# The recovery sums of a FitzHugh-Nagumo step: from GpSimd to ScalarE and VectorE

## The reference

```python
def cell(h, x):                       # layer 0, a GRU over time
    r, z = sigmoid(i_r + h_r), sigmoid(i_z + h_z)
    n = tanh(i_n + r * h_n)
    return (1 - z) * n + z * h
def _derivative(q, p, drive):         # layer 1, FitzHugh-Nagumo, DT = 0.01
    dq = q - q**3 / 3 - p + drive + tanh(q) @ coupling.T + bias
    dp = EPSILON * (q + ALPHA - BETA * p)
# one step: classical RK4 with four derivatives, then q and p are clipped to +-20; q is the output
x = x + gru(cond, x); x = x + fhn(cond, cond, x)
x = x + attention_over_blocks_and_layernorm(x)   # layer 2
x = x + grid_sample_1d(x, cond)                  # layer 3
```

## Time and profile before

| | |
|---|---|
| median of 3 runs | 3843.66 us (3839.34 to 3843.87) |
| the profiled execution | 3839.92 us, its span 3837.5 us |
| TensorE busy (matmul) | 3432.1 us, 89% |
| VectorE busy | 2881.2 us, 75% |
| ScalarE busy | 1870.0 us, 49% |
| GpSimd busy | 2035.7 us, 53% |
| mean granted TensorE clock | 0.845 |

### The profile page before, as it was taken

The page is one execution under the profiler, slowest core; times in us unless marked ns, Lnnn a source line. Parts: engine busy times, 40 slices in busy tenths (PEclk is TensorE's granted clock), DMA queues, the critical chain, the costliest instruction groups (busy, mean ns, idle before and its releaser), DMA issues.

```text
span 3837.5 us, 283786 instructions
## 1 busy us (share of the span) xinstructions
PE 3432.1 (89%) x115469; PEld 3184.2 (83%) x115469; DVE 2881.2 (75%) x17626; ACT 1870.0 (49%) x14495; POOL 2035.7 (53%) x7721
## 2 busy tenths in 40 slices
PE   8988998999999989999999998998999998999977
PEld 4478888888888888888888888888888888888853
DVE  2077777777777777777777777777777777777766
ACT  3245555555555555555555555555555555555543
POOL 0045555555555555555555555555555555555532
PEclk9998888888888888888888888888888888888778
DMA  3000000000000000000000000000000000000001
GB/s 121 22 24 1 1 1 1 1 1 1 1 1 1 1 1 1 1 1 1 1 1 1 1 1 1 1 1 1 1 1 1 1 1 1 1 1 1 1 1 44
DMA packets 9333, 23.44 MB, mean 6 GB/s; under 512 B 556, under 2 KB 600, under 8 KB 8792
## 3 DMA queue, kind: packets, MB, share of 16 engines
q1 hardware_dynamic: 8832, 19.92, 1.4%
q10 hardware_dynamic: 88, 0.02, 0.0%
HBM read 15.75 MB, written 4.19 MB: 5 GB/s over the span
## 4 chain that ended last, share of the span: by engine, by line
PE 80%; DVE 14%; issue 4%; ACT 1%; DVEq 0%; DMA 0%; ACTq 0%; POOL 0%
PE psum L1065 43%; PE psum L1045 31%; PE psum L1017 4%; DVE qnext L811 4%; DVE tpart L771 3%; DVE zdiff L739 2%; PE psum L1165 1%; DVE h L747 1%; DVE psum L811 0%; DVE sq L781 0%; DVE wih L884 0%; DVE q L820 0%; ACT tpart L517 0%; DVE wih L938 0%; DVEq L810 0%
## 5 line engine op out<-in xcount | busy, mean ns | idle before, releaser
L1065 PE MATMUL psum<-tpart,cpl 128*128 128x32 f16 x65536 | 2046.6, 180 | 346.6 <-DVE tpart L771 342.9
L1065 PEld LDWEIGHTS psum<-tpart,cpl 128*128 128x128 f16 x65536 | 1853.8, 98 | 450.4 <-DVE tpart L771 402.0
L1045 PE MATMUL psum<-hpart,whh 128*128 128x32 f16 x49152 | 1507.1, 181 | 7.6 <-DVE hpart L702 7.6
L1045 PEld LDWEIGHTS psum<-hpart,whh 128*128 128x128 f16 x49152 | 1381.2, 99 | 8.5 <-issue 6.2
L517 ACT ACTIVATE tpart<-psum 128x8 f16<-128x8 f32 x3072 | 525.0, 179 | 1127.0 <-DVE psum L811 1045.4
L771 DVE SCALAR_TENSOR_TENSOR tpart<-tfull,tpart 128x8 f16<-128x8 f32 x4096 | 735.1, 183 | 192.9 <-ACT tfull L519 162.6
L811 DVE TENSOR_REDUCE psum<-psum 128x8 f32<-128x24 f32 x3072 | 535.3, 189 | 401.2 <-PE psum L1065 241.3
L389 POOL TENSOR_TENSOR term<-coef,qhat 128x48 f32<-128x48 f32 (+1 forms) x1024 | 276.4, 270 | 511.1 <-ACT qhat L524 510.0
L519 ACT ACTIVATE tfull<-psum 128x8 f32<-128x8 f32 x3072 | 510.0, 175 | 0.0
L401 POOL TENSOR_TENSOR pn<-sums,qhat 128x16 f32<-128x16 f32 x511 | 113.4, 222 | 558.2 <-ACT qhat L524 558.2
L524 ACT ACTIVATE qhat<-psum 128x16 f32<-128x16 f32 x1536 | 324.3, 211 | 0.0
(11 more groups left out here) (148 smaller groups left out, 3602.4 us busy)
## 6 DMA issues: line engine op xcount, KB each, us to landing
xrow<-in_x_dram SPq DMA_DIRECT2D x4, 1024.0 KB, 11.3
out_dram<-space SPq DMA_DIRECT2D x16, 256.0 KB, 2.0
wih<-in_L_cond_W_ih_dram SPq DMA_DIRECT2D x3, 1024.0 KB, 9.6
space<-in_L_cond_W_hh_dram SPq DMA_DIRECT2D x1, 3072.0 KB, 18.7
space<-in_L_cond_coupling_dram SPq DMA_DIRECT2D x1, 1024.0 KB, 19.2
xrow<-in_cond_dram SPq DMA_DIRECT2D x1, 1024.0 KB, 4.8
wih<-in_L_cond_Wk_dram SPq DMA_DIRECT2D x1, 1024.0 KB, 5.4
wih<-in_L_cond_Wo_dram SPq DMA_DIRECT2D x1, 1024.0 KB, 7.7
```

Source lines behind the costliest of these rows:

```text
L1045: mm = pe.matmul(gate_out[part][:, :, :, col:col + B], whh[:, w, k, n * P:(n + 1) * P], copies_in(hpart[:, k, :, :]), start=(col == 0 and ...
L1065: mm = pe.matmul(stage_out[a][:, :, :, col:col + B], cpl[:, w, k, n * P:(n + 1) * P], copies_in(tpart[:, s % 2, k, :, :]), start=(col == 0 ...
```

## The change

GpSimd's work in the loop is given to the two other engines. ScalarE makes each product of the sums by one `Copy` with a constant scale (16 elements each): 4 from `phat`, 4 from `q1`, 3, 2 and 1 from the state in PSUM of stages 0, 1 and 2 (the one `Copy` `qhat` of each stage goes), and the scaled drive. VectorE does all additions, the clip of p, the drive and the output. `coef` and its memsets go. The clip of q becomes two instructions, of another form, one into PSUM and one into SBUF; `cub` and the square of stage 0 lie in PSUM. In stage 3, `base` and `sum_z` change places.

```diff
 # ScalarE
+            def stage_terms(s):
+                for r in range(s + 1, 4):
+                    ins = act.activation(in_halves(qterm[:, s + 1, r, :]), qt, ACT.Copy, scale=STEP[s] * sums_of[r][s + 2])
+                ins.then_inc(qterm_ready[s + 1], 1)
+            def first_terms(v):
+                act.wait_ge(phat_ready, v)
+                for r in range(4):
+                    ins = act.activation(pterm[:, r, :], phat[:, :], ACT.Copy, scale=sums_of[r][0])
+                ins.then_inc(pterm_ready, 1)
+                act.wait_ge(q1_ready, v)
+                for r in range(4):
+                    ins = act.activation(qterm[:, 0, r, :], q1[:, :], ACT.Copy, scale=STEP[3] * sums_of[r][1])
+                ins.then_inc(qterm_ready[0], 1)
+            def scaled_drive(v):
+                act.wait_ge(x1_ready, v)
+                act.activation(uscaled[:, :], x1[:, (v - 1) % 2, :], ACT.Copy, scale=k_c).then_inc(uscaled_ready, 1)
...
+                        if tail <= T:
+                            first_terms(tail)
                         act.wait_ge(q1_ready, tail)
...
                     if s == 1 and gru <= T:
                         gate_input(gru, tail)
                         sigmoid_r(gru)
+                    if s == 1 and tail <= T:
+                        scaled_drive(tail)
 # VectorE
             def clip(v):
+                dve.wait_ge(stage_sum[3][1], v)
+                if v < T:
+                    dve.scalar_tensor_tensor(clipped, qnext[:, :], clampq[:, 0:1], lowest,
+                                             ALU.min, ALU.max).then_inc(clipped_ready, 1)
...
-                dve.tensor_scalar(q1[:, :], qnext[:, :], clampq[:, 0:1], clampq[:, 1:2],
-                                  ALU.min, ALU.max).then_inc(q1_ready, 1)
+                dve.wait_ge(qterm_ready[0], v)
+                dve.scalar_tensor_tensor(q1[:, :], qnext[:, :], clampq[:, 0:1], lowest,
+                                         ALU.min, ALU.max).then_inc(q1_ready, 1)
...
+            def add_terms(s, v):
+                dve.wait_ge(qterm_ready[s], v)
+                if s == 0:
+                    dve.wait_ge(sums0_ready, v)
+                    dve.tensor_tensor(sums[:, :, :], pterm[:, :, :], qterm[:, 0, :, :], ALU.add).then_inc(sums_ready[0], 1)
+                else:
+                    dve.wait_ge(sums_ready[s - 1], v)
+                    dve.tensor_tensor(sums[:, s:4, :], sums[:, s:4, :], qterm[:, s, s:4, :],
+                                      ALU.add).then_inc(sums_ready[s], 1)
...
                 cubic(1, now)
+                first_sums(now)
+                if t >= 1:
+                    new_x(t - 1)
+                add_terms(0, now)
                 base(1, now)
+                if tail <= T:
+                    drive_sum(tail)
...
                 cubic(2, now)
+                add_terms(1, now)
                 base(2, now)
                 if gated_step:
                     sum_nr(gru)
+                if tail <= T:
+                    drive_scaled(tail)
                 sum_stage(2, 0, now)
...
                 cubic(3, now)
+                add_terms(2, now)
                 if gated_step:
                     difference(gru)
+                base(3, now)
+                if gated_step:
                     sum_z(gru)
-                base(3, now)
+                if tail <= T:
+                    add_last(now)
                 sum_stage(3, 0, now)
                 if gated_step:
                     weigh(gru)
+                if tail <= T:
+                    clip_p(tail)
                 sum_stage(3, 1, now)
...
                 clip(now)
                 if tail <= T:
+                    first_drive(tail)
                     split_tanh(0, 1, tail, tanh_ready[3][0], now)
```

More of the change, by code:

```diff
@@ L167, in build @@
         stage_base = psum[:, bank:2 * bank].rearrange("p (a c) -> p a c", a=HALVES)[:, :, 0:HC]
+        scratch_at = bank + 2 * HC
+        cub, square0, clipped, lowest = [psum[:, scratch_at + i * KB:scratch_at + (i + 1) * KB] for i in range(4)]
         stage3 = [triple(0, half), triple(bank + half, half)]
@@ L261, in build @@
         sq_ready = [sem(f"sq_ready{s}") for s in range(4)]
-        qhat_ready = [sem(f"qhat_ready{s}") for s in range(4)]
+        qterm_ready = [sem(f"qterm_ready{s}") for s in range(4)]
+        pterm_ready, clipped_ready = sem("pterm_ready"), sem("clipped_ready")
         cub_ready = [sem(f"cub_ready{s}") for s in range(4)]
         base_ready = [sem(f"base_ready{s}") for s in range(4)]
-        term_ready = [sem(f"term_ready{s}") for s in range(4)]
         sums_ready = [sem(f"sums_ready{s}") for s in range(4)]
@@ L326, in _ @@
                                pattern=[[-1, P]], channel_multiplier=1).then_inc(ident_ready, 1)
-            sums_of = recovery_sums()
-            for src in range(4):
-                for r in range(4):
-                    pool.memset(coef[:, src, r, :], sums_of[r][src] * (STEP[3] if src == 1 else 1.0))
             pool.iota(feature[:, :], pattern=[[-P, K]], base=0, channel_multiplier=-1,
@@ L407, in _ @@
-            for t in range(T):
-                step(t)
-            new_x(T - 1)
             pool.wait_ge(gi_mm, GROUPS)
@@ L753, in _, with drive_sum @@
                 link(ins)
+            def drive_sum(v):
+                dve.wait_ge(h_ready, v)
+                if v >= 3:
+                    dve.wait_ge(x2_ready, v - 2)
+                dve.tensor_tensor(x1[:, (v - 1) % 2, :], xT[:, v - 1, :, :].rearrange("p k b -> p (k b)"), h[:, :],
+                                  ALU.add).then_inc(x1_ready, 1)
             for v in (1, 2):
@@ L764, in _ @@
                 dve.wait_ge(h_ready, v)
+                if v == 1:
+                    drive_sum(1)
             h_high(3)
@@ new lines, in clip, with drive_scaled @@
+                dve.scalar_tensor_tensor(q1[:, :], qnext[:, :], clampq[:, 0:1], lowest,
+                                         ALU.min, ALU.max).then_inc(q1_ready, 1)
+            link(dve.memset(lowest, 1.0))
+            link(dve.tensor_scalar(lowest, lowest, clampq[:, 1:2], None, ALU.mult))
+            dve.tensor_copy(clipped, q1[:, :]).then_inc(clipped_ready, 1)
+            def drive_scaled(v):
+                dve.wait_ge(uscaled_ready, v)
+                dve.tensor_tensor(uhat[:, :], uscaled[:, :], bhat[:, :], ALU.add).then_inc(uhat_ready, 1)
@@ new lines, in first_drive, with new_x, first_sums @@
+            def first_drive(v):
+                dve.wait_ge(uhat_ready, v)
+                dve.wait_ge(phat_ready, v)
+                dve.tensor_tensor(drive0[:, :], uhat[:, :], phat[:, :], ALU.subtract).then_inc(drive0_ready, 1)
+            def new_x(t):
+                dve.wait_ge(q1plain_ready, t + 1)
+                dve.tensor_tensor(xT[:, t, :, :].rearrange("p k b -> p (k b)"), x1[:, t % 2, :], q1plain[:, :],
+                                  ALU.add).then_inc(x2_ready, 1)
+            def first_sums(v):
+                dve.wait_ge(pterm_ready, v)
+                dve.tensor_tensor(pterm[:, 0:3, :], pterm[:, 0:3, :],
+                                  uhat[:, :].unsqueeze(1).broadcast_to([P, 3, KB]), ALU.add).then_inc(sums0_ready, 1)
@@ new lines, in add_last, with clip_p @@
+            def add_last(v):
+                dve.wait_ge(qterm_ready[3], v)
+                dve.wait_ge(sums_ready[2], v)
+                dve.tensor_tensor(pn[:, :], sums[:, 3, :], qterm[:, 3, 3, :], ALU.add).then_inc(pn_ready, 1)
+            def clip_p(v):
+                dve.wait_ge(pn_ready, v - 1)
+                dve.tensor_scalar(phat[:, :], pn[:, :], clampc[:, 0:1], clampc[:, 1:2],
+                                  ALU.min, ALU.max).then_inc(phat_ready, 1)
+            drive_scaled(1)
@@ L823, in _ @@
+            first_drive(1)
             square(1)
@@ L880, in _ @@
                 step(t)
+            new_x(T - 1)
             dve.wait_ge(x2_ready, T)
```

100 lines of the change are left out of this document (24 added, 76 removed).

## The result

The changed kernel takes **4378.16 us** (4 runs, 4376.91 to 4379.42) against 3843.76 us before (4 runs, 3839.34 to 3844.16). The ratio is 1.1393, with a 95% interval of 1.1374 to 1.1413: slower by 534 us, where 4370 was forecast. The whole difference is in the loop. Between two first half-sums of stage 0 there are on average 7.86 us after and 6.82 before, and 511 times 1.04 is 531 us.

The account below looks back on a forecast made before the run. TensorE bound the kernel before, 86% of a step's chain; afterwards mostly VectorE and ScalarE. Six legs sum to 7.69 us, taken as 7.85, 1.03 above 6.82; 511 steps give 526 us more: 4370 us, range 4150 to 4550.

Parts of the forecast that it names:

- A: From stage 0's second half-sum to stage 1's first, through ScalarE's products and VectorE's cubic and additions: 1.74 us, before 1.40.
- B: From stage 1's first half-sum to stage 2's, which is queued behind an addition waiting for ScalarE: 2.10 us, before 1.61.
- D: From stage 3's first half-sum to its second, through sum_z, the sigmoid, weigh and clip_p: 0.71 us, before 0.30.
- the allowance for small waits: Over the whole step, the walk gives some 2% too little, so 7.69 us was taken as 7.80.
- The stall at L799: Between stages 1 and 2, VectorE stands still about 0.5 us ahead of drive_scaled, with stage 2's half-sum queued behind.
- The queue waits at 0.10 instead of 0.03: On VectorE, a late semaphore waited for in the queue costs 0.10 us, not 0.03; five waits, bound -0.35 a step.
- The wide additions at 0.20 and 0.22: VectorE's additions of 48 and 64 elements take 0.20 and 0.22 us; bounds -0.08 to +0.11 a step.
- `clip_p` and the hold: Ahead of stage 3's second half-sum, clip_p holds its follower 0.28 us; bound -0.08 if only 0.20 counts.
- Relief: Rival: GpSimd no longer slows VectorE and the additions fit its free time; 102 us faster, 3740 us; chance 4%.
- Only the tail pays: Rival: TensorE stays the bound in stages 1 and 2, only the tail gets longer; 153 us, 3990 us; chance 9%.
- ScalarE as the bound: Rival: nine tail copies at 0.21 us, not 0.11, delay stage 0's tanh by 0.75; 4750 us; chance 6%.
- VectorE at 85% or more: Sign expected in the profile after: VectorE's busy share at 85% or more.

Follow-up runs that it names:

- experiments 1 and 2: experiment 1, and a second run: the changed kernel with paired waits exchanged, so the late semaphore is waited for by the instruction itself; 4114.17 us.
- experiment 1: The changed kernel with only drive_scaled moved, from ahead of the half-sum of stage 2 to behind the cubic of stage 3; 4169.85 us.
- experiment 4: The kernel before with only the clip of q in its new form, a scalar_tensor_tensor with one pointer scalar; 3795.92 us.
- experiment 8: The kernel before with one added wait: GpSimd starts the products and sums of phat behind the second split of tanh; 3758.23 us.
- experiment 3: The changed kernel with GpSimd doing five additions and products per step on its own data, which nobody waits for; 4443.97 us.

## Why the prediction was right, step by step

The legs, as means over the steps of the profiled execution, beside the walk:

```
leg                                      walked  measured
A  2nd half-sum st. 0 -> 1st of stage 1    1.74    1.84
B  -> 1st half-sum of stage 2              2.10    2.23
C  -> 1st half-sum of stage 3              1.48    1.53
D  -> 2nd half-sum of stage 3              0.71    0.62
E  -> second split of tanh                 0.68    0.63
F  -> 2nd half-sum of stage 0              0.98    1.02
sum                                        7.69    7.87
taken, with the clock                      7.85
```

**The sum.** It came out within 0.02 of what was taken, and partly because errors cancel: A, B, C and F together were 0.32 short, D and E 0.14 long, and the allowance for small waits was 0.11. That the total is so close is in part luck. The median step is 7.80; the mean is pulled up by some 100 steps of 8.0 to 8.15.

**A and B, the chain through two engines.** The mechanism is shown by experiments 1 and 2. The shortfall is in the ScalarE part: in the step above its operations from PSUM start 0.06 to 0.08 apart, and the third product of stage 0 ends 0.78 after the second half-sum's start (walked: 0.72); the second product of stage 1 ends 0.84 after it (0.80). VectorE's starts behind the cubic and the base of stage 2 were 0.11 where 0.09 was taken.

**The stall at L799.** Walked as about 0.5 of standing still; it is 0.39, 510 times. Its price in the time, 208 us, is what experiment 1 took away.

**The queue waits at 0.10 instead of 0.03.** Read from one kind of row before, and right: 0.09 to 0.11 after, 0.03 to 0.04 with the waits exchanged. I had kept -0.35 a step in the bounds for them; exchanging them is worth -0.50, since the wait of `weigh` in D is a sixth one, and the starts behind two of them came 0.02 closer.

**The wide additions at 0.20 and 0.22.** All of them after, by shape, mean ns behind the busy time:

```profile
L824 DVE TENSOR_TENSOR sums<-pterm,qterm 128x64 f32<-128x64 f32 x512 | 115.5, 226 | 10.8 <-issue 1.2
L827 DVE TENSOR_TENSOR sums<-sums,qterm 128x48 f32<-128x48 f32 x512 | 106.8, 209 | 2.3 <-issue 2.3
L816 DVE TENSOR_TENSOR pterm<-pterm,uhat 128x48 f32<-128x48 f32 x512 | 103.5, 202 | 1.7 <-issue 1.7
```

The rule of the Trainium skill that the prediction set beside its own numbers (page "VectorE: DVE Perf Modes", the TRN2 errata) gives 207 and 224 ns, and by these rows it is the better one: 202 and 209, and 226.

**`clip_p` and the hold: the step that failed.** I had written that what follows a tensor_scalar with two pointer scalars starts or ends 0.28 behind it, read from the split of the earlier trace rows that ended at 302.07 and took 0.25. After, the half-sum behind `clip_p` starts 0.20 later, the mean of all steps too. The operation is long (289 ns) but holds its follower only 0.20. The 0.25 of the split was GpSimd's doing: experiment 4 removes the tensor_scalar and the split becomes 0.28, experiment 8 keeps it and only makes GpSimd wait, and the split takes 0.17. D came out 0.09 shorter than walked, 0.08 of it by this. The end of the range at -0.08 ("if only its start distance of 0.20 counts") was the truth.

**Relief.** The rival's cause is real and its size as stated: the contention costs about 0.13 where it falls (0.14 in experiment 3, 0.13 on the square in 8). What it could not do is pay for 0.4 in A and 0.5 in B. The time it named, 3740 us, is near what experiment 8 gets (3758) by moving GpSimd's products and leaving the rest alone, but not for its reason: the rival had 102 us from shorter steps, and there only 24 come so and the rest goes with the clock. The exclusion of VectorE and GpSimd that the Trainium skill states (page "SBUF — State Buffer", section "SBUF: two separate sides") agrees in direction with 171 ns becoming 311 in experiment 3, beside GpSimd operations of about 330 ns (128x64). The splits there also have two SBUF inputs and ran beside GpSimd at 0.15 to 0.16 us; that is not what a lock on every such pair would give, and no run here settles why.

**Only the tail pays, ScalarE as the bound.** The first fell with A, 0.42 longer than before, and B, 0.55. Against the second, the products of p and of q take 0.52 for four (557.27 and 557.69 in the step shown), so 0.11 from start to start, and ScalarE is 54% busy.

**VectorE at 85% or more, TensorE's waits.** The first is wrong: 309 of 400 us, 77%. That number had no sum behind it. Lengths added up leave out the overlap: instructions that start 0.09 to 0.15 apart and are 0.16 to 0.23 long cover less than the sum of their lengths. TensorE's waits came, about 0.15 ahead of stage 2, 0.42 ahead of stage 3 and about 0.8 ahead of stage 0, not over 1.2. The wait ahead of stage 0 had no sum behind it. It ends with the first split, which depends on the first half-sum and stands in VectorE's queue behind the second. D is 0.31 longer than before, but that split now starts 0.18 behind the second half-sum where it was 0.26, and takes 0.16 where it took 0.22, so the wait grew by only about 0.2 us. GpSimd at 1% and the chain on VectorE and ScalarE are as said.

## What to carry to other kernels

When work is moved from an idle engine to a chain of small operations, walk the chain start by start: the busy share tells nothing (VectorE had 19% free in the earlier trace rows, and the time rose by 14%). Before moving anything, ask which operation is queued behind the one that waits, and which of two semaphores comes last. An engine off the critical path can still be in the way of one on it; making it wait gave 2.1% here, most of it with the clock, and taking it out of the loop cost 1.1% even with the order mended, or 0.20 us a step (3%) if steps at full clock are compared.
